# Six tiles of rows from SyncE instead of seven, the seventh gathered by GpSimd

## What is computed

```python
emb = jax.vmap(lambda tbl, idx: tbl[idx], in_axes=(0, 1), out_axes=1)(embed_tables, sparse)
bi = emb[:, FIRST, :] * emb[:, SECOND, :]
a = jax.nn.relu(jnp.einsum('bpd,dh->bph', bi, att_w_w) + att_w_b)
scores = jnp.einsum('bph,ho->bpo', a, att_d_w) + att_d_b
att_weight = jax.nn.softmax(scores, axis=1)
att_out = jnp.sum(att_weight * bi, axis=1)
x = jnp.concatenate([att_out, dense], axis=-1)
out = jax.nn.sigmoid(x @ fin_w + fin_b)
```

## Time and profile before

| | |
|---|---|
| median of 3 runs | 469.24 us (468.34 to 469.72) |
| profiled execution | 468.43 us |
| its span | 466.6 us |
| TensorE matmul busy | 399.1 us (86%) |
| VectorE busy | 395.3 us (85%) |
| GpSimd busy | 332.4 us (71%) |
| ScalarE busy | 129.7 us (28%) |
| mean granted TensorE clock | 0.955 |
| DMA | 15.46 MB, mean 33 GB/s |

### The profile page before, as it was taken

One profiled execution on the slowest core, in us unless ns is written; L12 is line 12 of the kernel. 1 busy time (PEld: TensorE's weight loads), 2 busy tenths in 40 slices (PEclk: granted clock), 3 DMA queues, 4 the chain that ended last, 5 costly groups with the idle time before them and its releaser, 6 DMA issues.

```text
span 466.6 us, 9661 instructions
## 1 busy us (share of the span) xinstructions
PE 399.1 (86%) x2508; PEld 223.0 (48%) x2508; DVE 395.3 (85%) x641; ACT 129.7 (28%) x302; POOL 332.4 (71%) x349
## 2 busy tenths in 40 slices
PE   1696969999898987899898899699998899699674
PEld 1585746544336654354326766345326755352121
DVE  4999798999768886999795988899796997898765
ACT  3203311242342111142352121042263111125163
POOL 5877777777777777777777777777777777777600
PEclk9978879999999999799999999899999999899988
DMA  8558323222222222232112243323112223322200
GB/s 294 90 151 161 26 13 26 17 26 15 14 15 26 27 15 26 14 26 16 15 15 15 28 22 27 15 26 16 15 15 14 14 13 17 13 16 16 14 1 1
DMA packets 16535, 15.46 MB, mean 33 GB/s; under 512 B 8192, under 2 KB 15584, under 8 KB 16096
## 3 DMA queue, kind: packets, MB, share of 16 engines
q0 software_dynamic: 11040, 5.67, 23.0%
q1 hardware_dynamic: 3056, 6.80, 4.2%
q10 hardware_dynamic: 2384, 2.37, 2.1%
HBM read 14.79 MB, written 0.02 MB: 32 GB/s over the span
## 4 chain that ended last, share of the span: by engine, by line
SPq 69%; issue 25%; PE 2%; DVE 2%; DMA 1%; ACT 1%; ACTq 0%
SPq L401 56%; SPq L397 13%; DMA index<-look_index 1%; PE sums_s L506 1%; DVE ring L850 1%; PE sums_f L492 0%; PE first L482 0%; ACT shared L682 0%; DMA emb_placed<-tables 0%; PE back L530 0%; PE back L522 0%; SPq L379 0%; ACT shared L607 0%; ACT shared L622 0%; ACT shared L601 0%
## 5 line engine op out<-in xcount | busy, mean ns | idle before, releaser
L431 POOL DMA_INDIRECT emb<-tables,rows x300 | 283.7, 946 | 91.5 <-issue 90.6
L850 DVE TENSOR_TENSOR ring<-emb_t,turned 128x512 f32<-128x512 f32 (+9 forms) x180 | 191.7, 1099 | 0.3
L465 PE MATMUL looked_own<-look_parts,onehot 128*128 128x448 f32 x546 | 125.8, 383 | 9.4 <-DVE look_masked L835 4.5
L465 PEld LDWEIGHTS looked_own<-look_parts,onehot 128*128 128x128 f32 x546 | 104.1, 195 | 39.2 <-issue 22.5
L482 PE MATMUL first<-ring,par 128*32 128x512 f32 (+1 forms) x672 | 89.2, 608 | 29.6 <-DVE ring L850 29.0
L594 ACT ACTIVATE hidden<-first,par 128x512 f32<-128x512 f32 (+1 forms) x84 | 56.5, 677 | 175.7 <-PE first L482 175.2
L492 PE MATMUL sums_f<-ring,par 128*32 128x512 f32 (+1 forms) x672 | 89.0, 598 | 0.0
L465 PE MATMUL back<-look_parts,onehot 128*128 128x448 f32 x350 | 79.8, 380 | 10.1 <-DVE onehot L750 6.1
L465 PEld LDWEIGHTS back<-look_parts,onehot 128*128 128x128 f32 x350 | 65.9, 194 | 29.6 <-issue 14.4
L750 DVE TENSOR_TENSOR onehot<-chunk_of,turned 128x896 fp32r<-128x896 f16 x60 | 63.1, 1052 | 0.0
L826 DVE STREAM_TRANSPOSE emb_t<-emb 128x128 f32<-128x128 f32 x100 | 29.9, 302 | 35.0 <-DMA emb<-tables,rows 19.2
(11 more groups left out here) (75 smaller groups left out, 134.2 us busy)
## 6 DMA issues: line engine op xcount, KB each, us to landing
emb_placed<-tables SPq DMA_DIRECT2D x896, 0.1 KB
emb<-tables,rows POOLq DMA_INDIRECT x300, 3.5
ring<-tables SPq DMA_DIRECT2D x2, 1568.0 KB, 9.7
shared<-tables SPq DMA_DIRECT2D x1, 1568.0 KB, 7.8
chunk_of<-chunk_numbers ACTq DMA_DIRECT2D x12, 128.0 KB, 3.6
ring<-tables SPq DMA_DIRECT2D x1, 896.0 KB, 5.9
emb<-tables,rows_first POOLq DMA_INDIRECT x44, 3.8
ring<-tables SPq DMA_DIRECT2D x1, 672.0 KB, 7.3
```

The lines of the kernel that those rows point to most:

```text
L431: pool.indirect_dma_start(emb[:, f, g * D:(g + 1) * D], None, stacked, bass.IndirectOffsetOnAxis(ap=row, axis=0), element_offset=at,).then ...
L465: mm = nc.tensor.matmul(looked_rows[look_bank[tile]], onehot[:, tile % ONEHOTS, c, :], look_parts[:, n, c, k, :], start=c == 0 and k == 0, ...
L850: nc.vector.tensor_tensor(slot[:, at:at + n, :], emb_t[:, i:i + n, :], turned[f % 2][:, 0, :].unsqueeze(1).broadcast_to((P, n, P)), ALU.mu ...
```

## The change

`TILES_SP` goes from `(1, 2, 2, 2)` to `(1, 2, 2, 1)`. SyncE fetches one of the two placed tiles of the last quad instead of both, the second one (tile 15 of the batch, i = 1). GpSimd gathers the first (tile 14, i = 0), together with the placed tile of quad 0, ahead of field 13 in quad 0.

```diff
--- before.py
+++ after.py
@@ -17,7 +17,7 @@
 BATCH = 4
 ROWS_SP = 32
 SP_FIELD = 24
-TILES_SP = (1, 2, 2, 2)
+TILES_SP = (1, 2, 2, 1)
 PLACED = 2
 SP_PLACE = 23
 SP_FIRST = 13
```

## The result

The changed kernel takes 464.17 us (median of 4 runs, 463.98 to 464.57) beside 469.28 us for the kernel before in the same comparison. The ratio is 0.9895, with a 95% interval of 0.9878 to 0.9912: 4.9 us less (4.1 to 5.7). Forecast were 464.5 us and a range of 462.7 to 466.2. The profiled execution is one of 463.98 us with a span of 462.1; forecast was a span of 461.9.

What follows compares the result with a forecast made beforehand. It took SyncE's last row, which lands late and leaves VectorE standing still for 4.00 us, to bound the kernel. -5.97 + 1.25 = -4.72 us from the median of 469.24 gave 464.5 us, range 462.7 to 466.2.

Steps and rivals of the forecast that it cites:

- What ended last: Last quad: SyncE's last row lands at 444.40, ScalarE's placed copy waits for it, and VectorE stands still 4.00 us.
- The 5.97 us: Last quad: without SyncE's late row VectorE's early maximum starts 5.97 us earlier, before the added gather's delay.
- third quad's chain: Same steps with rows already there: the score copy ends 4.75 us after the last products start; taken for the last quad.
- The 1.25 us of the gather: GpSimd's added gather makes all 300 gathers behind it 1.25 us later, and VectorE with them; paid once.
- The bound of 2.45: Upper limit of the added gather's price: 2.45 us if it is one of the long gathers among the first 44.
- An unbroken row of work: Last quad: VectorE works on unbroken after its last gather wait at 401.80, so the 1.25 us reach field 23 whole.
- Cover of the other arrivals: Last quad: field 25's last gather lands by 444.1, VectorE asks for it at 447.5; 3.3 us to spare.
- Shorter landings: With SyncE silent from 381, gathers near 400 land sooner, up to 1.7 us gained: 462.8; chance 0.13 with costless gather.
- A free gather: GpSimd's added gather costs nothing: 463.3 us; chance 0.13, shared with sooner landings.
- Slower by TensorE's clock: With products 1.25 us later, TensorE meets low clock stretches elsewhere; at most 10.6 us, 475.1; chance 0.03.

Runs made afterwards that it cites:

- before_3spare: The kernel before with three spare GpSimd gathers, into a buffer nothing reads, ahead of field 13 of quad 0: 467.84 us, ratio 0.9973.
- after_again: The changed kernel, unaltered, measured once more in a second comparison: 463.37 us, ratio to the kernel before 0.9872.
- gpsimd_takes_both: The changed kernel with GpSimd gathering both placed tiles of the last quad, one gather more: 465.20 us, ratio to the kernel before 0.9917.
- field_25: The kernel before, SyncE's seven tiles fetched for field 25 instead of 24, ScalarE's placed copy one field later: 462.91 us, ratio 0.9863.
- no_row_at_all: The changed kernel without its added gather, that tile fetched by nobody (zeros stand there): 462.27 us, ratio to the kernel before 0.9862.
- seventh_tile_96_rows: The kernel before with SyncE fetching only 96 of the 128 rows of its seventh tile, no gather added: 462.05 us, ratio 0.9848.

## Why the prediction held

**What ended last.** SyncE's last row, by the 4.00 us of VectorE's gap. Shown: three spare gathers do not slow the kernel before and speed it only through that gap, the spare matmuls leave its time as it was, and a seventh tile that ends at 428 costs nothing.

**The 5.97 us.** Built from the third quad's chain at full clock. The early maximum moved by -5.94 once the gathers' +1.44 are set apart, and the chain from the last products to the end of the score copy took 4.76 us (446.53 - 441.77) for the 4.75 of the third quad. The gap itself is 4.0 us of it, and the other 1.9 are TensorE's and ScalarE's backlog and the low clock: from field 24 turned to L890 it was 6.21 us before (451.06 - 444.85) and is 4.32 now (446.56 - 442.24). before_3spare, which keeps SyncE's row but not the gap, has 4.62. Of the 1.6 us between 6.21 and 4.62, 1.40 lie between the starts of L601 and L622 (5.19 us before, 3.79 in before_3spare), in the same work: the matmuls shown above took 1.11 and 1.94 us in place of 0.66 and 1.06. So most of the 1.6 is the clock, and the term came out right because the third quad's times were made at a full one.

**The 1.25 us of the gather.** The mechanism held: every later gather 1.50 us late, VectorE 1.44. Of this 1.25 is the gather; the rest comes from the first 44 gathers, one long one above all, whose sum went from 47.6 to 48.2 us, while the 300 behind them gave 0.3 back (283.7 to 283.4). Those 44 are the same in all kernels, and their sum was anything from 47.0 to 48.3, so it comes with the execution and not with the change. Two single traces can therefore miss the price by as much as it is: the last gather is issued between 439.12 and 441.21 in the six kernels with no gather added and between 440.72 and 441.76 in the five with one. The means of the two groups, 440.13 and 441.42, differ by 1.29 us, which is the 1.25. The bound of 2.45 was too wide a worry and the size of 1.25 right.

**"An unbroken row of work" behind the last gather wait.** This step of the prediction was right in its result and too simple in its reason. VectorE's stretch is not of one length: it took 26.4 to 26.5, 28.1 or 28.8 to 29.4 us, going with the granted clock from 402 to 412, by its waits for ScalarE's copies (0.3 to 0.5, 2.1 or 2.8 us). Before and after had the same 28.1 in the two profiled executions, so it fell out of the difference; that was luck, as after_again with its 29.4 shows, where the early maximum moved by 3.47 us and not 4.50. I had the low clock as a rival for slowness from 425 on and missed that it stood at 402 to 412 in the kernel before, where it costs 1.6 us against a full clock. The two profiled executions of the changed kernel differ by 1.04 us (463.98 and 465.02), and all of it arises in this stretch (28.14 and 29.36 us, less 0.18 of the gathers); for its other executions, from 462.70 us on, no trace shows the cause.

**Cover of the other arrivals.** Field 25's gathers were not asked for too early, as said. The prediction did not weigh those of fields 22 and 23, which were covered only by the low clock ahead of them: VectorE waits for them in all five traces with a full clock from 402 to 412.

**The rivals.** Shorter landings: out, by a landing that does not go with SyncE in fourteen traces. A free gather: out by the means of the traces and by gpsimd_takes_both. Slower by TensorE's clock: not seen; the clock rose where the gap had been.

**Open.** The size of the gather's price over the runs. The changed kernel lies 0.4 us above field_25 and 1.5 and 2.2 us above no_row_at_all and seventh_tile_96_rows by its first comparison (0.5 and 1.1 by its second), with intervals of about a microsecond to each side; moving the gather to the last quad won nothing; three spare gathers cost 2.5 or 3.6 us where 3.75 were expected. The forecast was of 4.72 us less: the first comparison (4.9) bears it out, the second (6.0, 5.0 to 6.9) is above it, so the last 0.3 us of agreement are luck. field_25 is faster than before and does all the work with no gather more, but that it beats the changed kernel (0.9863 against 0.9872, the same comparison) is not shown.

## What to carry to other kernels

When the chain of waits names a queue that never rests, look for the engine that stands still at its end: what a shorter queue gives is that engine's gap and the backlog behind it, not the length of the queue, and a twin of the same stage that meets no wait gives the size. A delay that is put into a pacing queue early is carried to the last place where somebody waits for that queue, and that place can move (field 14 here, field 23 once the clock was full); adding spare work on both sides of the change (hidden before, paid after) shows which queue holds the end. Before moving work to another engine, see whether the late result can be asked for later: giving SyncE the next field's rows took the wait away here too, with no work moved.

## What the hardware showed that I had not expected

More work made a kernel faster: three spare gathers took 1.3 us off the kernel before, by shortening a gap of TensorE, behind which the granted clock had been 0.53. In all four kernels that had them, sixteen spare matmuls in a gap that is 3.4 to 4.1 us long without them went with a granted clock of 1.00 for the 10 us behind it, where the kernels without them showed 0.50 to 0.79 in one of the stretches 402 to 407 and 407 to 412, except seventh_tile_96_rows, which had a gap of 3.9 us and a full clock behind it. So a gap of this size is followed by a low clock in most executions and not in all. The Trainium skill's "TensorE: Matmul & The Clock Gate", Part 1, says that idleness throttles the engine and that the warm-up is run-variable; the traces agree with both. And SyncE's single-row copies, 128 in 62 us, did not delay GpSimd's gathers by anything that stood out of the 0.4 us by which the landing varies between traces. The Trainium skill's "DMA: Bandwidth & Descriptors", under "Queues, rings and completion order", says that an engine takes turns between the queues that have work for it; no price of that for the gathers is seen here.
